# A GNN layer with a residual and a layer norm: the projected table p kept as two float32r words in place of three bfloat16 words, and its split moved from GpSimd to ScalarE and VectorE

## The chip, the cores and the metric

The kernel runs on one core of a Trainium2 chip. The metric is device time in microseconds (us), one launch, the median of the runs shown. Engines are named as in the profile: PE is TensorE (PEld its weight loads), ACT is ScalarE, DVE is VectorE, POOL is GpSimd, SP is SyncE, which here only issues DMAs.

## The reference, cut to what matters

```python
# x (12500, 256), src and dst (200000,), edge_weight (200000,), 4 heads, DO = 64
def head(w1, bb1, w2, bb2, a1, aab1, a2, aab2):
    feats = jnp.maximum(x @ w1 + bb1, 0.0) @ w2 + bb2            # (12500, 64)
    x_cat = jnp.concatenate([feats[src], feats[dst], edge_weight[:, None]], axis=1)   # 129 wide
    hid = jnp.maximum(x_cat @ a1 + aab1, 0.0)                    # (200000, 129)
    e1 = jax.nn.leaky_relu((hid @ a2 + aab2)[:, 0], negative_slope=0.2)
    w = jnp.exp(e1 - jnp.max(e1))
    pooled = segment_sum(w[:, None] * feats[dst], src)
    row_sum = segment_sum(w, src) + 1e-10
    return pooled / row_sum[:, None]
out = layernorm(x + concatenate_heads(vmap(head)(...)))
```

`x_cat @ a1` is a sum of three parts, p[src] + q[dst] + weight * a_row. With 4 heads p and q have ZW = 4 * 129 = 516 columns. p holds the bias `aab1`, and each is made once for each node and not once for each edge.

## The kernel before

**Nodes and windows.** The 12500 nodes are 100 windows of WN = 125. A table `p_table` has p, another, `qf_table`, has q and the features (QW = 776 columns, float32). Every edge belongs to the window of its source node.

**First part, to about 400 us.** Weights and edges are loaded, and the edges are counted by window.

**The sort loop (`sort_loop`, 26 groups, of which 25 make nodes).** A group is 16 steps q = 0 to 15, on each engine in an order written out by hand. It handles four blocks of 2000 edges and at the same time makes p, q and the features of four windows. For the sort, each step has on PE a prefix sum (`prefix`, L823) and placing products (`place`, L834), on ACT the one-hot rows of windows (`windows`, L1051 and L1056), on DVE `pick` (L1398) and `chunks` (L1433). Once in four steps DVE has `split` and `slots` (L1407 to L1423) and `row_ids` (L1442), and POOL scatters the rows of a block with three indirect DMAs (`scatter`, L695). For the nodes PE has `hidden` (L857, q = 1 to 8), `feats` (L866, q = 3 to 9), `q_product` (L888, q = 10 to 13) and `p_product` (L877, q = 11, 13, 15 and 1 of the group after). Both p_products of a window write psum banks 5 and 6. DVE's `p_sum` (L1454, same steps as `p_product`) adds the bias and writes p to `p_f`. POOL's `split_p` (L706 to L713) makes three bfloat16 words of it in four instructions, and SP stores them. PE's next `p_product` waits for `p_sum` of the last one:

```python
def p_product(g, w):
    ...
    since(pe, s_p_ev, n)
    for q in range(2):
        mm = pe.matmul(psum[0:WN, 5 + q, 0:HALF], f_t[:, q, at], ad_p[:, q, :], start=True, stop=True)
```

PE's order at q = 1 is prefix, turned rows, place, `p_product` of the window before, `hidden(0)`. PE may run two prefixes ahead of DVE's `pick` and no further. DVE's order in a step is split, pick, slots, row_ids, chunks, and then what stands beside.

**The tables.** After the sort, windows of tiles are packed into a table `win_pack`, `end_prev` holds where windows end, and the sorted fields are turned into `records`.

**The edge loop (`pipeline`, 208 superblocks of 8 tiles of 128 edges, 1664 tiles).** For each tile POOL gathers 128 rows of `qf_table` (L754) into one of 24 slots. PE's `hidden_src` makes p[src]: a one-hot matrix of 128 x 128 (`onehot_t`, bfloat16) times the window's p (`p_win`, three words, 258 columns at a time), so six products (L971). Then the identity times the gathered half, in float32 (L975). `turn` transposes one-hot matrices (L984, four at a time), after `hidden_src(2)` for the second half of this superblock and after `hidden_src(6)` for the first half of the next. `sum_up` (L958, float32) sums the weighted features. ACT's `take_turned` (L1182) copies the transposed matrices to `onehot_t`, twice a superblock. ACT also builds one-hot matrices (`onehots`, L1193 to L1197) and weights features (`weight`, L1164, four heads for each tile). ACT's order in a superblock is take_turned, onehots, exps, weight(0), take_turned, weight(1) to (3), weight(4), onehots, weight(5) to (7). `hidden_src(0)` and `hidden_src(4)` wait for take_turned. DVE adds p and q (L1558), has four dot products (L1568), sums up (L1617) and some small steps once a superblock (L1582 to L1624).

SP loads the p of a window while the one before it is in work (`p_win` has two places). The last 100 us are the division, the residual and the layer norm.

Of the kernel before, what the change touches and what calls it, by code (L numbers as in the profile page):

```python
# [25 lines left out]
I32 = mybir.dt.int32  # L26
BF16 = mybir.dt.bfloat16
AX_X = mybir.AxisListType.X


def gnn_layer(nc, x, src, dst, weight, W1, b1, W2, b2, A1, ab1, A2, ab2, out):
# [50 lines left out]
    p_table = nc.dram_tensor("p_table", (N, 3 * ZW), BF16, kind="Internal").ap()  # L82
# [7 lines left out]
    with ctx:  # L90
# [12 lines left out]
        ones_b = sb("ones_b", [P, P], BF16)  # L103
        before = sb("before", [P, P], BF16)
        iota_row = sb("iota_row", [P, WN])
        iota_win = sb("iota_win", [P, CH, W], BF16)
# [4 lines left out]
        onehot_t = sb("onehot_t", [P, SB, P], BF16)  # L111
# [10 lines left out]
        decay = sb("decay", [P, SPB, H])  # L122
        shift_all = sb("shift_all", [P, NSB, H])
        last_sb = sb("last_sb", [P, W], I32)
        end_prev = sb("end_prev", [1, W], I32)
        win_pack = sb("win_pack", [1, NT // 4], I32)
# [4 lines left out]
        row_tmp = onehot_t[0:1, :, :].rearrange("p t n -> p (t n)").bitcast(I32)[:, 0:NT // 4]  # L131
# [66 lines left out]
        dst_part = edge_row.bitcast(I32)  # L198
        hist_m = base_hl[:, 0:2 * HG * HCOL * LO].rearrange("p (b m c n) -> p b m c n", b=2, m=HG, c=HCOL)
# [90 lines left out]
        s_tab_step = sem("s_tab_step")  # L290
        s_acc_zero = sem("s_acc_zero")
# [191 lines left out]
        def _(sp):  # L483
# [1248 lines left out]
```

## Time and profile before

| what | value |
|---|---|
| median of 3 runs | 4876.15 us (4874.23 to 4877.1) |
| span of the profiled execution | 4828.3 us |
| median less span | 47.85 us |
| busy share PE, DVE, ACT, POOL | 88%, 92%, 79%, 56% |
| sort loop, from one group to the next | 52.3 us |
| edge loop, three superblocks | 45.27 us |

The span is the time from the first to the last instruction that the profile holds. What lies around it, start and end of the launch, is in the runs' times and not in the span; of the profiled execution only the span is on record. A busy PE isn't PE at its peak, since the end of a matmul is modelled: the distance between two starts says more than the duration.

### The profile page before, as it was taken

How to read it: one execution, taken by the hardware profiler on the slowest of the kernel's cores; microseconds unless marked ns; L12 is line 12 of the kernel's file. 1: busy time of each engine (PE TensorE's matmuls, PEld its weight loads, DVE VectorE, ACT ScalarE, POOL GpSimd, SP SyncE). 2: the span in 40 equal slices, each digit the busy share in tenths (PEclk: the TensorE clock that was granted, in tenths of full speed). 3: DMA queues.
4: the chain of work that ended last, by engine and by line, in shares of the span. 5: the costliest groups of instructions: out<-in, count | busy, mean ns of one | idle time of the engine just before them, and what ended most of it. 6: DMA issues, size and time to landing. Idle time of an engine off the chain costs nothing.

```text
span 4828.3 us, 133194 instructions
## 1 busy us (share of the span) xinstructions
PE 4260.4 (88%) x24114; PEld 3004.1 (62%) x24115; DVE 4460.2 (92%) x25378; ACT 3835.5 (79%) x12983; POOL 2693.5 (56%) x2886
## 2 busy tenths in 40 slices
PE   1598998898896999999999999999999999999990
PEld 1355555555555777777777777777777777777760
DVE  8799999999996999999999999999999999999998
ACT  1587778778774888888888888888888888888884
POOL 5366666666664555555555555555555555555544
PEclk9999999999997999999999999999999999999995
DMA  2133333333334877777777777777777777777757
GB/s 85 43 73 86 79 71 80 81 77 80 79 76 137 240 225 221 228 225 224 224 225 224 225 225 221 226 224 224 225 224 224 224 225 225 225 225 225 221 172 212
DMA packets 266918, 851.82 MB, mean 176 GB/s; under 512 B 107916, under 2 KB 109584, under 8 KB 266861
## 3 DMA queue, kind: packets, MB, share of 16 engines
q0 software_dynamic: 169920, 673.54, 50.0%
q1 hardware_dynamic: 63543, 160.18, 11.2%
q10 hardware_dynamic: 33398, 17.49, 1.4%
q8 instruction: 18, 0.29, 0.0%
q14 instruction: 39, 0.32, 0.0%
HBM read 739.10 MB, written 111.90 MB: 176 GB/s over the span
## 4 chain that ended last, share of the span: by engine, by line
PE 36%; ACT 27%; issue 3%; DVE 2%; DMA 1%; ACTq 0%; POOL 0%; DVEq 0%; SPq 0%; POOLq 0%
ACT z L1164 18%; PE psum L971 15%; PE psum L975 9%; PE psum L958 8%; ACT onehot L1193 3%; ACT onehot_t L1182 3%; PE psum L984 3%; ACT onehot L1197 2%; PE psum L939 1%; DVE z L1689 1%; DVE z L1682 0%; PE psum L995 0%; ACT onehot L1195 0%; DVE z L1705 0%; DMA p_win<-p_table 0%
## 5 line engine op out<-in xcount | busy, mean ns | idle before, releaser
L754 POOL DMA_INDIRECT z<-qf_table,rec x1664 | 1609.2, 967 | 1454.9 <-PE psum L958 1027.1
L1164 ACT ACTIVATE z<-z 128x64 f32<-128x64 f32 x6656 | 1651.1, 335 | 0.0
L971 PE MATMUL psum<-p_win,onehot_t 128*128 x9984 | 1407.8, 274 | 84.1 <-ACT onehot_t L1182 68.3
L971 PEld LDWEIGHTS psum<-p_win,onehot_t 128*128 128x128 bf16 x9984 | 966.8, 97 | 540.0 <-issue 214.4
L958 PE MATMUL psum<-z,onehot 128*128 128x260 f32 x3328 | 1029.4, 391 | 6.7 <-DVE acc L1617 4.9
L975 PE MATMUL psum<-z,ident 128*128 128x258 f32 x3328 | 1002.7, 383 | 0.0
L1568 DVE SCALAR_TENSOR_TENSOR z<-z,a_b 128x129 f32<-128x129 f32 x3328 | 884.3, 290 | 5.6 <-issue 0.2
L1568 DVE SCALAR_TENSOR_TENSOR z<-psum,a_b 128x129 f32<-128x129 f32 x3328 | 828.2, 286 | 0.0
L1558 DVE TENSOR_TENSOR z<-z,psum 128x258 f32<-128x258 f32 x1664 | 698.6, 420 | 94.6 <-PE psum L975 90.6
L1617 DVE TENSOR_TENSOR acc<-acc,psum 125x260 f32 x1664 | 702.3, 422 | 25.3 <-PE psum L958 2.4
L695 POOL DMA_INDIRECT sorted_rows<-z x300 | 478.5, 1595 | 403.9 <-DVE z L1447 321.6
L958 PEld LDWEIGHTS psum<-z,onehot 128*128 128x128 f32 x3328 | 575.8, 190 | 103.1 <-DVE acc L1617 27.7
L1182 ACT ACTIVATE onehot_t<-psum 128x512 bf16<-128x512 f32 x416 | 243.4, 585 | 437.7 <-PE psum L984 437.7
L1193 ACT ACTIVATE onehot<-iota_row,rec 128x125 f32<-128x125 f32 x1664 | 525.5, 389 | 26.3 <-PE psum L958 22.7
L1051 ACT ACTIVATE z<-iota_win,z 125x100 bf16<-125x100 bf16 x1600 | 470.3, 369 | 71.3 <-DMA base_rows<-z 56.3
L1433 DVE TENSOR_SCALAR acc<-z 125x320 bf16<-125x320 bf16 x1600 | 521.1, 388 | 0.3 <-issue 0.3
L975 PEld LDWEIGHTS psum<-z,ident 128*128 128x128 f32 x3328 | 502.2, 190 | 20.3
L857 PE MATMUL psum<-acc 128*128 128x500 f32 x800 | 377.8, 594 | 5.6 <-ACT acc L1085 5.6
L1398 DVE SCALAR_TENSOR_TENSOR z<-psum,z 125x100 f32<-125x100 f32 x1600 | 319.5, 253 | 24.1 <-PE psum L823 24.0
L984 PE MATMUL psum<-ident,onehot 128*128 128x128 f32 x1664 | 261.5, 280 | 55.7 <-ACT onehot L1197 55.7
L1197 ACT ACTIVATE onehot<-onehot,ones_f 128x500 f32<-128x500 f32 x416 | 298.2, 717 | 0.0
L1091 ACT ACTIVATE acc<-psum,acc 128x500 f32<-128x500 f32 x200 | 135.3, 676 | 196.0 <-PE psum L857 195.9
(220 smaller groups left out, 5576.3 us busy)
## 6 DMA issues: line engine op xcount, KB each, us to landing
p_table<-acc SPq DMA_DIRECT2D x100, 338.6 KB
p_win<-p_table SPq DMA_DIRECT2D x100, 338.6 KB
z<-qf_table,rec POOLq DMA_INDIRECT x1664, 4.5
qf_table<-acc SPq DMA_DIRECT2D x75, 339.5 KB
acc<-in_x_dram SPq DMA_DIRECT2D x25, 448.0 KB
z<-in_x_dram SPq DMA_DIRECT2D x20, 560.0 KB
out_dram<-z ACTq DMA_DIRECT2D x20, 560.0 KB
qf_table<-z SPq DMA_DIRECT2D x25, 339.5 KB
```

What stands on the lines that cost most here:

```text
L695: pool.indirect_dma_start(out=sorted_rows, out_offset=bass.IndirectOffsetOnAxis(ap=row_i[0:KB[k], (b - 3) % 2, k:k + 1], axis=0), in_=rows ...
L754: pool.indirect_dma_start(out=z_t[:, o + j, :], out_offset=None, in_=qf_table, in_offset=bass.IndirectOffsetOnAxis(ap=rec[:, o + j, 3:4].b ...
L958: pe.matmul(psum[:, 4 + j % 2, 0:H * HF], onehot[:, slot, :], z_t[:, slot, ZW:QW], start=True, stop=True)\
L971: mm = pe.matmul(to, onehot_t[:, j, :], p_flat[:, bass.ds((w % 2) * (3 * ZW) + (part * ZW + o), n)], start=(part == 0), stop=(part == 2 an ...
L975: mm = pe.matmul(z_two(slot), ident[:, :], z_t[:, slot, NA:ZW], start=False, stop=True, skip_group_check=True)
L1051: op = act.activation(win_oh[0:EP, b % 2, c, :], iota_win[0:EP, 0, :], ACT.Abs, scale=-1.0, bias=edge_win[0:EP, bass.ds((g * PER + b) * CB ...
L1164: op = act.activation(z_t[:, slot, o:o + DO], z_t[:, slot, o:o + DO], ACT.Copy, scale=z_t[:, slot, o + DO:o + HF])
L1193: op = act.activation(onehot[:, oo + j, 0:WN], iota_row[:, :], ACT.Abs, scale=-1.0, bias=rec[:, oo + j, 0:1])
L1433: op = dve.tensor_scalar(chunk_oh[0:EP, r, c, :], iota_k[0:EP, :], chunk_f[0:EP, c:c + 1], None, ALU.is_equal)
L1558: dve.tensor_tensor(own, own, z_one(slot), ALU.add).then_inc(s_z_added, 1)
L1568: return dve.scalar_tensor_tensor(out=own, in0=of, scalar=0.0, in1=a2_b[:, h * AT:(h + 1) * AT], op0=ALU.max, op1=ALU.mult, accum_out=e_ra ...
L1617: dve.tensor_tensor(a, a, psum[0:WN, 4 + j % 2, 0:H * HF], ALU.add).then_inc(s_acc, 1)
```

## The change

* p is stored as two float32 words: ACT copies the product from PSUM into `p_out` as float32r (`high_part`), and DVE subtracts that word from the same PSUM (`p_low`). `p_sum`, `p_f` and POOL's `split_p` go.
* The bias comes in by one more product for each half, a column of ones (one row) times the bias row, in float32.
* `high_part` is at ACT's steps q = 12, 14 and 0, 2 of the group after, behind `windows`; `p_low` last in DVE's steps of the same numbers. `p_sum` was at q = 11, 13, 15, 1.
* In the edge loop the one-hot matrix is written as float32r and p is multiplied in two words: four products for a tile in place of six.
* `p_win`, `p_table` and `onehot_t` get larger: 1032 words of 4 bytes for a node in place of 1548 of 2 bytes. To make room, `win_pack` and `end_prev` are built in z and copied by one DMA into a free row of `acc` after ACT's last zeroing of `acc`; other constants move to z.
* The row `a_row`, which stands below p in `p_win`, is split in two steps and not in five.

```diff
-        p_win = sb("p_win", [P, 2, 3 * ZW], BF16)
+        p_win = sb("p_win", [P, 2, 2 * ZW], F32R)
-        onehot_t = sb("onehot_t", [P, SB, P], BF16)
+        onehot_t = sb("onehot_t", [P, SB, P], F32R)
...
+        tables = acc[WN:WN + 1, 0:NT // 4 + W]
...
             def store_p(g, w):
-                sp.wait_ge(s_p_lo, g * 4 + w + 1)
+                sp.wait_ge(s_p_ev, g * 4 + w + 1)
...
             sp.wait_ge(s_tab_step, N_TAB_STEPS)
+            sp.wait_ge(s_acc_zero, 1 + BULK)
+            sp.dma_start(tables, tables_made).then_inc(s_tab_st, 16)
             sp.wait_ge(s_rec_st, 16 * BULK)
...
-            def split_p(g, w):
...
-                pool.tensor_copy(p_out[0:WN, b, 0:ZW], pf).then_inc(s_p_hi, 1)
...
-                pool.tensor_tensor(pf, pf, p_out[0:WN, b, 0:ZW], ALU.subtract).then_inc(s_p_rest, 1)
...
-            order = [(split_p, -1, 3), (scatter, 0, 0), (scatter, 0, 1), (scatter, 0, 2), (split_p, 0, 0), (split_p, 0, 1),
-                     (scatter, 0, 3), (split_p, 0, 2)]
...
                 for q in range(2):
-                    mm = pe.matmul(psum[0:WN, 5 + q, 0:HALF], f_t[:, q, at], ad_p[:, q, :], start=True, stop=True)
+                    pe.matmul(psum[0:WN, 5 + q, 0:HALF], f_t[:, q, at], ad_p[:, q, :], start=True, stop=False)
+                    mm = pe.matmul(psum[0:WN, 5 + q, 0:HALF], ones_f[0:1, 0:WN], ab1_b[0:1, q * HALF:(q + 1) * HALF], start=False, stop=True)
...
-                        for part in range(3):
-                            mm = pe.matmul(to, onehot_t[:, j, :], p_flat[:, bass.ds((w % 2) * (3 * ZW) + (part * ZW + o), n)],
-                                           start=(part == 0), stop=(part == 2 and not (o and PEH)), skip_group_check=True)
+                        for part in range(2):
+                            mm = pe.matmul(to, onehot_t[:, j, :], p_flat[:, bass.ds((w % 2) * (2 * ZW) + (part * ZW + o), n)],
+                                           start=(part == 0), stop=(part == 1 and not (o and PEH)), skip_group_check=True)
...
+            def high_part(g, w):
+
+                n, b = g * 4 + w, w % 2
+                act.wait_ge(s_p_mm, n + 1)
+                since(act, s_p_st[b], g * 64 + w // 2 * 32)
+                act.activation(p_out[0:WN, b, 0:ZW].bitcast(F32R).rearrange("p (q n) -> p q n", q=2), psum[0:WN, 5:7, 0:HALF], ACT.Copy).then_inc(s_p_hi, 1)
+
+            beside = {0: [(-1, high_part, 2), (0, take_x)], 1: [(0, take_h, 0)], 2: [(-1, high_part, 3), (0, take_h, 1)], 3: [(0, take_h, 2)],
+                      4: [(0, take_h, 3)], 5: [(0, take_h, 4)], 6: [(0, take_h, 5)], 7: [(0, take_f, 0), (0, take_h, 6)], 8: [(0, take_h, 7)],
+                      9: [(0, take_f, 1)], 10: [(0, take_q, 0)], 11: [(0, take_q, 1)], 12: [(0, high_part, 0), (0, take_q, 2)], 13: [(0, take_q, 3)],
+                      14: [(0, high_part, 1)]}
...
-            def p_sum(g, w):
+            def p_low(g, w):
 
                 n = g * 4 + w
-                dve.wait_ge(s_p_mm, n + 1)
-                since(dve, s_p_lo, n - 1)
-                dve.tensor_tensor(p_f[0:WN, w % 2, :].rearrange("p (q n) -> p q n", q=2), psum[0:WN, 5:7, 0:HALF],
-                                  ab1_b[0:WN, :].rearrange("p (q n) -> p q n", q=2), ALU.add).then_inc(s_p_ev, 1)
-
-            beside = {11: [(0, p_sum, 0)], 13: [(0, p_sum, 1)], 15: [(0, p_sum, 2)], 1: [(-1, p_sum, 3)]}
+                dve.wait_ge(s_p_hi, n + 1)
+                dve.tensor_tensor(p_out[0:WN, w % 2, ZW:].rearrange("p (q n) -> p q n", q=2), psum[0:WN, 5:7, 0:HALF],
+                                  p_out[0:WN, w % 2, 0:ZW].rearrange("p (q n) -> p q n", q=2), ALU.subtract).then_inc(s_p_ev, 1)
+
+            beside = {12: [(0, p_low, 0)], 14: [(0, p_low, 1)], 0: [(-1, p_low, 2)], 2: [(-1, p_low, 3)]}
```

## Rows read from the trace of the kernel before

**Rows 1.** Busy time by stage: window, length, PE, PEld, DVE, ACT, POOL, clock, DMA share, GB/s.

```profile
400.00:1480.00 1080.00, 965.76 (x3959) 552.97 (x3958) 1030.30 (x5193) 843.77 (x2280) 687.57 (x578) 0.98 0.36 79
```

**Rows 2.** The same for three superblocks of the edge loop.

```profile
3000.00:3045.27 45.27, 43.38 (x275) 32.83 (x274) 42.27 (x268) 38.77 (x145) 24.69 (x30) 1.00 0.75 220
```

**Rows 3.** Waits in the edge loop: total us, times, longest.

```profile
ACT onehot_t L1182 <- PE psum L984: 418.4, 203, 2.2
```

**Rows 4.** Timeline of the edge loop, ACT and PE: start, us, engine, line.

```profile
3002.54 0.60 ACT L1182 ACTIVATE onehot_t<-psum 128x512 bf16<-128x512 f32 x1 [2.19 <-PE psum L984]
...
3011.62 0.57 ACT L1182 ACTIVATE onehot_t<-psum 128x512 bf16<-128x512 f32 x1
...
3012.64 0.92 PE L971 MATMUL psum<-p_win,onehot_t 128*128 x6 [0.20 <-issue]
...
3014.26 0.82 PE L971 MATMUL psum<-p_win,onehot_t 128*128 x6
...
3014.93 0.60 PE L975 MATMUL psum<-z,ident 128*128 128x258 f32 x2
...
3015.36 0.60 PE L958 MATMUL psum<-z,onehot 128*128 128x260 f32 x2
...
3017.61 0.60 ACT L1182 ACTIVATE onehot_t<-psum 128x512 bf16<-128x512 f32 x1 [1.88 <-PE psum L984]
```

**Rows 5.** A group of weight loads, whole span: count, busy us, mean ns, idle before.

```profile
L975 PEld LDWEIGHTS psum<-z,ident 128*128 128x128 f32 x3328 | 502.2, 190 | 20.3
```

**Rows 6.** One DVE line from 400 to 1480 us: duration ns min/median/max.

```profile
L1433 DVE TENSOR_SCALAR acc<-z x1320: 286/298/1231, 401.1 to 1479.6; 125x320 bf16<-125x320 bf16 x189
```

**Rows 7.** Timeline of PE in the sort loop, steps q = 12 to 3.

```profile
1093.92 0.33 PE L823 MATMUL psum<-z,before 127*128 127x400 bf16 x1
...
1109.97 1.14 PE L877 MATMUL psum<-acc 128*125 128x258 f32 x4 [0.32 <-DVE acc L1454]
1110.94 1.84 PE L857 MATMUL psum<-acc 128*128 128x500 f32 x4
...
1116.73 0.33 PE L823 MATMUL psum<-z,before 127*128 127x400 bf16 x1 [1.54 <-DVE z L1398]
```

**Rows 8.** Timeline of DVE in the same steps.

```profile
1088.93 0.25 DVE L1398 SCALAR_TENSOR_TENSOR z<-psum,z 125x100 f32<-125x100 f32 x1
...
1090.51 0.25 DVE L1398 SCALAR_TENSOR_TENSOR z<-psum,z 125x100 f32<-125x100 f32 x1
...
1092.17 0.94 DVE L1433 TENSOR_SCALAR acc<-z 125x320 bf16<-125x320 bf16 x4
...
1094.73 0.16 DVE L1407 CAST z<-z 125x16 int32<-125x16 f32 x1
...
1095.49 0.26 DVE L1398 SCALAR_TENSOR_TENSOR z<-psum,z 125x100 f32<-125x100 f32 x1
...
1098.56 2.14 DVE L1433 TENSOR_SCALAR acc<-z 125x320 bf16<-125x320 bf16 x4
...
1108.37 0.94 DVE L1433 TENSOR_SCALAR acc<-z 125x320 bf16<-125x320 bf16 x4
1109.23 0.69 DVE L1454 TENSOR_TENSOR acc<-psum,acc 125x516 f32<-125x516 f32 x1
1109.83 0.16 DVE L1407 CAST z<-z 125x16 int32<-125x16 f32 x1
```

**Rows 9.** Timeline of ACT in the same steps.

```profile
1096.07 0.58 ACT L1103 ACTIVATE acc<-psum 125x516 f32<-125x516 f32 x1
...
1096.81 1.17 ACT L1051 ACTIVATE z<-iota_win,z 125x100 bf16<-125x100 bf16 x4
...
1098.58 0.60 ACT L1103 ACTIVATE z<-psum 125x516 f32<-125x516 f32 x1
```

**Rows 10.** Waits of SP's DMA queue from 1500 to 4600 us.

```profile
SPq L594 <- PE psum L975: 2238.1, 97, 28.5
SPq L596 <- DMA p_win<-p_table: 504.8, 98, 6.4
```

More of the change, by code:

```diff
@@ L27 @@
 BF16 = mybir.dt.bfloat16
+F32R = mybir.dt.float32r
 AX_X = mybir.AxisListType.X
@@ L215, in gnn_layer @@
         iota_s = carve_z(S // 2).bitcast(BF16)
+        iota_win = carve_z(W // 2).bitcast(BF16)
         ident_b = carve_z(P // 2).bitcast(BF16)
+        ones_b = carve_z(P // 2).bitcast(BF16)
+        before = carve_z(P // 2).bitcast(BF16)
         before_f = carve_z(P)
@@ L697, in scatter @@
                         in_=rows_out[0:KB[k], (b - 3) % 2, 2 * (W + 1) + k * SF:2 * (W + 1) + (k + 1) * SF], in_offset=None, compute_op=ALU.add).then_inc(s_scat, 16)
-            def split_p(g, w):
-                n, b = g * 4 + w, w % 2
-                pf = p_f[0:WN, b, :]
-                pool.wait_ge(s_p_ev, n + 1)
-                since(pool, s_p_st[b], g * 64 + w // 2 * 32)
-                pool.sem_inc(s_passed, 1)
-                pool.tensor_copy(p_out[0:WN, b, 0:ZW], pf).then_inc(s_p_hi, 1)
-                pool.wait_ge(s_p_hi, n + 1)
-                pool.tensor_tensor(pf, pf, p_out[0:WN, b, 0:ZW], ALU.subtract).then_inc(s_p_rest, 1)
-                pool.wait_ge(s_p_rest, n + 1)
-                pool.sem_inc(s_passed, 1)
-                pool.tensor_copy(p_out[0:WN, b, ZW:2 * ZW], pf).then_inc(s_p_mid, 1)
-                pool.wait_ge(s_p_mid, n + 1)
-                pool.tensor_tensor(p_out[0:WN, b, 2 * ZW:3 * ZW], pf, p_out[0:WN, b, ZW:2 * ZW], ALU.subtract).then_inc(s_p_lo, 1)
-            order = [(split_p, -1, 3), (scatter, 0, 0), (scatter, 0, 1), (scatter, 0, 2), (split_p, 0, 0), (split_p, 0, 1),
-                     (scatter, 0, 3), (split_p, 0, 2)]
             def group(g):
-                for work, off, n in order:
-                    if work is scatter and isinstance(g, int) and g * PER + n - 3 == BLOCKS - 1:
+                for n in range(PER):
+                    if isinstance(g, int) and g * PER + n - 3 == BLOCKS - 1:
                         pool.wait_ge(s_sum, 4 * BLOCKS)
                         pool.iota(win_iota, [[P, NT]], base=0, channel_multiplier=0, allow_small_or_imprecise_dtypes=True).then_inc(s_win_iota, 1)
-                    if (live_b(g, n, -3) if work is scatter else not isinstance(g, int) or 0 <= g + off < GROUPS):
-                        work(g + off, n)
+                    if live_b(g, n, -3):
+                        scatter(g, n)
             sort_loop(pool, group)
@@ L1050, in windows @@
                 for c in range(j * CH, (j + 1) * CH):
-                    op = act.activation(win_oh[0:EP, b % 2, c, :], iota_win[0:EP, 0, :], ACT.Abs, scale=-1.0,
+                    op = act.activation(win_oh[0:EP, b % 2, c, :], iota_win[0:EP, :], ACT.Abs, scale=-1.0,
                                         bias=edge_win[0:EP, bass.ds((g * PER + b) * CB + c, 1)])
@@ L1121, in group @@
                         take_rows(g, b)
-                    for work, *args in beside.get(q, []):
-                        if not isinstance(g, int) or g < GROUPS:
-                            work(g, *args)
+                    for off, work, *args in beside.get(q, []):
+                        if not isinstance(g, int) or 0 <= g + off < GROUPS:
+                            work(g + off, *args)
             act.dma_start(base_rows_d[:, :, :].rearrange("h u n -> h (u n)"), base_hl[0:BLOCKS, :].bitcast(BF16)).then_inc(s_base_st, 16)
@@ L1146, in _ @@
                                psum[:, g % 2 * 6 + 1, 0:3 * P].rearrange("p (f t) -> p t f", f=3), ACT.Copy).then_inc(s_field_b, 1)
-                act.activation(acc[:, g * part:(g + 1) * part], zero_col[:, :].to_broadcast([P, part]), ACT.Copy).then_inc(s_acc_zero, 1)
+                act.activation(acc[0:WN, g * part:(g + 1) * part], zero_col[0:WN, :].to_broadcast([WN, part]), ACT.Copy).then_inc(s_acc_zero, 1)
             act.wait_ge(s_start, 1)
```

74 lines of the change are left out of this document (31 added, 43 removed).

## The prediction

> **What bounds the kernel now.** I read the busy time by stage first, then the timelines of one cycle of each big loop, and the waits last. There are two loops, bound in two ways.
>
> The sort loop takes 52.3 us a group. In it DVE is busy 1030 of 1080 us, PE 966, ACT 844, POOL 688 [rows 1]. So DVE is the fullest engine. Part of that isn't work: `chunks` (L1433) takes 298 ns at the median and up to 1231 [rows 6]. Four of them take 0.94 us where POOL is quiet and 2.14 where the timeline has POOL in `split_p` [rows 8]. All 1320 have 431 us where 330 fours at 0.94 would have 310, so 121 us in 20.6 groups, about 5.9 us a group, nearly all of it beside GpSimd's own instructions. The group has two halves. From q = 3 to q = 11 PE runs almost without a gap (eight `hidden`, eight `feats`). From q = 12 to q = 2 DVE sets the pace and PE waits for it. With the prefix of q = 12 as zero (1093.92), the last `p_product` starts at 16.05, `hidden(0)` at 17.02 and the prefix of q = 3 at 22.81 [rows 7]. The rest to 52.3, that is 29.5 us, is PE's half.
>
> The edge loop takes 45.27 us for three superblocks, 15.09 each, with PE busy 43.4, DVE 42.3, ACT 38.8 [rows 2]. The two fullest aren't the whole story. ACT waits 203 times, 2.06 us each, for PE's `turn` (L984): once a superblock [rows 3]. That shows a cycle. From the copy L1182 at 3002.54 ACT works without a stop up to the end of the next one at 3012.19 (9.65 us). PE then starts `hidden_src(4)` at 3012.64, and three tiles and a `turn` later ACT's next copy starts at 3017.61 (4.97 us) [rows 4]. Together it is 15.07 us, the whole superblock. What makes PE's part shorter shortens the superblock, up to DVE's 42.27 / 3 = 14.09 us busy.
>
> **Edge loop: four products in place of six.** Six bfloat16 products of 258 columns take 0.67 us from start to start (3014.26 to 3014.93), 0.11 each. A float32 product of 258 columns is two matmuls and takes 0.43 (3014.93 to 3015.36) [rows 4]. No float32r product is in the trace. Below it is bounded by the bfloat16 price, 0.11, since the columns have to stream; above by the float32 one, 0.43; between them lies one float32 matmul of the two, 0.215. I take 0.11: a word that holds part of float32's digits, two of which are to give the whole, asks for one pass like a bfloat16 word, of which three give the whole. A four-byte weight load is 190 ns long [rows 5], but two of them and their two matmuls fit into 0.43, so a load hides behind 0.215 at least.
>
> So 4 x 0.11 = 0.44 for 0.67, 0.22 less a tile. In the cycle stand three tiles of PE's part, 3 x 0.22 = 0.66, which gives 14.4. DVE's 14.09 busy leaves 0.3 for its own gaps, so I take 14.5: 0.59 x 205 superblocks = 121 us less. Bounds of this term: 137 less, if all of 0.66 is had; 60 less, if DVE's waits stay; with 0.215 for a product, three tiles are 3 x 0.2 longer, which gives 15.7 and 125 us more; with 0.43 PE has 1.05 us more a tile, and 1700 us are added.
>
> The Trainium skill speaks against my price ("TensorE: Matmul & The Clock Gate", sections on back-to-back gaps, weight loads and fast weight load): the distance of matmuls in a real stream comes from load and matmul together, a load of 128 columns takes about 107 ns, the fast load isn't for FP32, and loads overlap running matmuls only in other row groups. If load and stream added up, four products would take some 0.86 us in place of 0.43, an estimate from that page. The trace disagrees for float32, where pairs with loads take 0.43 and would take more.
>
> ACT's copy to `onehot_t` reads 512 float32 columns as before; 125 x 516 written as float32 take 0.58 [rows 9], this one as bfloat16 0.57 to 0.60 [rows 4]: nothing. The window's p is a third larger. SP's load takes 504.8 / 98 = 5.15 us and is waited for by SP alone, which before that waits 2238 / 97 = 23 us for PE to be through with a window [rows 10]. 6.9 us still fit; if a window were short, 1.7 us more would show. Nothing.
>
> **Sort loop: what goes.** POOL's four instructions, and with them most of the 5.9 us of stretched `chunks`. POOL's scatters stay and stretch some. The stores wait for DVE now, later by less than a step.
>
> **Sort loop: what comes.** PE: two one-row products of 258 columns for each `p_product`. Columns count, so 0.43 each, 0.86 a `p_product` and 3.4 a group (bounds 0 and 1.14, the whole L877 group [rows 7]). DVE: `p_low` is as wide as `p_sum`, 0.60 from start to start [rows 8]. ACT: `high_part`, 0.50 to 0.58 as L1103 [rows 9]. But where they stand matters more. `p_product` waits for `p_low` of the last one, which stands a step later than `p_sum` did and behind ACT. I walk DVE's half again, prefix of q = 12 at zero, with quiet prices: split 0.76, pick and slots 3.07 (1095.49 to 1098.56), chunks 0.86, pick and row_ids 1.66 (1090.51 to 1092.17), a plain step 1.58 [rows 8]; windows 1.77, take_q 0.74 [rows 9].
>
> * q = 12: pick at 0.4, chunks end 4.3, `p_low(0)` 4.9. ACT: `high_part` delays take_q by 0.5, and `q_product(3)` runs 3.65 to 5.05. So `p_product(1)` 5.05 to 6.8.
> * PE's prefix of q = 14 is behind it. DVE's q = 13 ends at 6.5, so it waits until 7.2, ends the step at 8.8 and waits for `high_part(1)`, which ACT reaches at 8.5. `p_low(1)` ends at 9.7, `p_product(2)` at 11.5.
> * DVE: q = 15 ends at 12.2, q = 0 with split, pick, slots and chunks at 16.9, `p_low(2)` at 17.5. Only then comes `p_product(3)`, 17.55 to 19.3. Before it started at 16.05. Behind it on PE are `hidden(0)` (to 21.0), the prefix of q = 2, and `hidden(1)`.
> * The prefix of q = 3 comes at 23.4; before 22.81, where it waited 1.54 for DVE, and that wait goes.
>
> PE's half has `p_product(0)`, 0.86 longer: 29.5 + 0.86 = 30.3. The group is 53.7 us. I add 0.2 for scatters that still stretch DVE: 53.9, so 1.6 more a group, in 24 groups 38 us more. The freed DVE time isn't used because PE waits in the middle of the steps, not at their ends. Bounds: PE's busy time before is 966 / 1080 x 52.3 = 46.8 us a group [rows 1]; if the group shrank to that, it would be 132 us less in all. With two of the hops a microsecond later each, 85 more.
>
> For the stretching, the Trainium skill ("SBUF — State Buffer", who interferes with whom) says VectorE and GpSimd share a port pair which the one that comes first holds whole. The trace agrees: 2.14 for 0.94. `p_low` reads PSUM and one SBUF operand, which by that page doesn't contend.
>
> **The rest.** The copy of the tables is issued when ACT's last zeroing ends, ahead of the load of the first records, which waits for their store; I put 1 us. The split of `a_row` has three steps less under other waits: nothing, 1 us if it weren't.
>
> **The sum** against the profiled execution: 4828.3 - 121 + 38 + 1 = 4746. Median less span is 47.85, as before: 4794, some 82 us or 1.7% less than the median of 4876.15.
>
> **The rivals.**
>
> 1. *The sort loop gains too.* For it: DVE is fullest there, and 5.9 us a group go. Against: the walk above, in which PE waits for `p_low(2)`. If DVE's relief let PE run without waits, PE's 46.8 + 3.4 = 50.2 us would be the group, 2.1 less, and the time 4876 - 121 - 50 = 4705; at the bound of 46.8 it would be 4623.
> 2. *float32r costs one float32 matmul or more* (slower). Place: L971, four times a tile. For it: operands are four bytes wide and the weight load is 190 ns. Against: only that a word with part of the digits should need one pass. From 0.165 us a product on, four cost as much as six. At 0.215: 4876 + 125 + 39 = 5040; at 0.43 some 6600.
> 3. *The edge loop doesn't shorten.* Something else holds 15 us, as DVE's busy 14.09 with its waits for `turn` and maxima, or the loads of four-byte weights just eat the gain. For it: DVE is within 7%. Against: ACT's regular wait for PE [rows 3]. Then 4876 + 39 = 4915.
>
> **How the numbers follow.** My forecast 0.62, by itself 4740 to 4860; rival 1 0.13; rival 2 0.12; rival 3 0.13. A tenth of the forecast's own range would be within 0.2% or slower. Less than 0.2%, 10 us, I count as the same, about what a measurement of this kernel can tell from no change. Faster: 0.13 + 0.58 + 0.02 of rival 3 = 0.73; same 0.06; slower 0.21. Left out of the range are rival 2, the upper part of rival 3 and the far end of rival 1: 4680 to 4890. Its upper end takes in the forecast with both terms at their worse bounds within reason (60 less and 85 more, with 1, would be 4902).
>
> **What would show it.** L971 four times a tile at 0.11 from start to start, 14.5 us a superblock, ACT's wait for L984 down by about 0.6 and DVE's for L975 near zero. In the sort loop `chunks` back at 0.94 for four, groups of 53.9 us, and PE's L877 waiting for DVE's `p_low` by microseconds at q = 1, where before it was 0.32 [rows 7]. Wrong would be: a start-to-start of L971 of 0.2, groups below 51 us, or DVE idle in the edge loop by more than 0.5 us a superblock.

## The result and the profile after

The changed kernel takes 5002.77 us (median of 4 runs, 4999.77 to 5004.83) where the kernel before takes 4875.31. The ratio is 1.0259, 95% interval 1.0244 to 1.0273: slower by 127 us. The forecast was 4794, its range 4680 to 4890, and it gave "slower" a chance of 0.21.

First the page of the changed kernel: its span, the busy time of each engine, and three of its costliest groups.

```profile
span 5000.4 us, 123442 instructions
PE 4248.6 (85%) x21186; PEld 3034.1 (61%) x21187; DVE 4276.9 (86%) x25375; ACT 3879.0 (78%) x13083; POOL 2365.6 (47%) x2486
L958 PE MATMUL psum<-p_win,onehot_t 128*128 x6656 | 1351.7, 325 | 150.5 <-issue 94.3
L1393 DVE SCALAR_TENSOR_TENSOR z<-psum,z 125x100 f32<-125x100 f32 x1600 | 320.9, 256 | 371.5 <-PE psum L809 368.4
L1428 DVE TENSOR_SCALAR acc<-z 125x320 bf16<-125x320 bf16 x1600 | 382.2, 302 | 0.8 <-issue 0.8
```

What was meant to go went: POOL is busy 47% of the span, and `chunks` (now L1428) takes 302 ns on average and four of them 0.94 us again. But `pick` (now L1393) waits 368 us for PE's prefix. The same two stretches as in [rows 1, 2] say where the time came from. The columns are busy times of PE, PEld, DVE, ACT, POOL, the granted clock, DMA share, GB/s.

```profile
400.00:1480.00 1080.00, 994.61 (x3699) 532.58 (x3698) 768.94 (x4483) 776.52 (x2060) 353.37 (x216) 0.92 0.33 76
3000.00:3045.27 45.27, 40.78 (x234) 32.98 (x232) 43.09 (x273) 39.82 (x150) 25.51 (x32) 1.00 0.79 237
```

In the sort loop DVE does 4483 instructions in the time in which it did 5185 to 5193, and PE has the lower granted clock, 0.92. A group takes 60.9 us (median of 24, mean 60.6) for 52.3 before: about 195 us more in 24 groups. The edge loop is shorter: 14.74 us a superblock (median) for 15.08. Here is the place in the sort loop, the timeline of PE from the prefix of q = 12 of one group to that of q = 3 of the next (L809 is `prefix`, L863 and L864 are `p_product` and its bias rows, L843 is `hidden`):

```profile
1054.99 0.34 PE L809 MATMUL psum<-z 127*128 127x400 bf16 x1
...
1060.05 0.70 PE L863 MATMUL psum<-acc 128*125 128x258 f32 x2 [0.76 <-DVE acc L1448]
1060.68 0.70 PE L864 MATMUL psum<-acc,ones_f 1*125 1x258 f32 x2
...
1062.56 0.34 PE L809 MATMUL psum<-z 127*128 127x400 bf16 x1
...
1065.27 0.70 PE L863 MATMUL psum<-acc 128*125 128x258 f32 x2 [0.54 <-DVE acc L1448]
...
1073.79 0.88 PE L863 MATMUL psum<-acc 128*125 128x258 f32 x2 [3.42 <-DVE acc L1448]
...
1078.05 3.40 PE L843 MATMUL psum<-acc 128*128 128x500 f32 x4
1081.28 0.33 PE L809 MATMUL psum<-z 127*128 127x400 bf16 x1
...
1083.69 0.33 PE L809 MATMUL psum<-z 127*128 127x400 bf16 x1
```

The reader is to see three things. `p_product(1)` with its bias takes 2.51 us from start to start (1060.05 to 1062.56). The last one waits 3.42 us for `p_low(2)` (L1448). After this wait it takes 4.26 us, and `hidden(0)` 3.23, where before the same four matmuls took 1.68. The same stretches in the view by windows (the granted clock is the third column from the end):

```profile
1054.00:1074.00 20.00, 15.27 (x75) 8.90 (x75) 15.99 (x82) 15.47 (x42) 8.42 (x6) 1.00 0.49 122
1074.00:1084.50 10.50, 10.50 (x27) 4.88 (x27) 2.99 (x22) 2.98 (x9) 0.00 (x0) 0.67 0.20 52
1084.50:1114.50 30.00, 29.80 (x113) 15.79 (x111) 24.22 (x149) 25.92 (x70) 11.69 (x8) 1.00 0.29 57
```

PE is busy for all of the second stretch, but at 1.2 GHz for about two thirds of it. Summed over 24 groups, PE's clock stands at this lower level for 236 us, 10.2 us in most groups and 6.8 in the one shown, which with 59.55 us is one of the shortest. All of it lies between the prefix of q = 12 and that of q = 3. In the first profile of before it is 55 us in all, 3.4 us in two groups of three, and these groups are no longer than the third (52.1 to 52.4 us, one 52.9, for 52.2 to 52.4): there DVE sets the pace.

### The profile page after: what moved, and what is told of

Read it like the earlier page. It is cut to its first block, busy times and chain, and to the rows that moved or that the text cites. A ratio compares the mean times of both kernels' runs of the same rounds, so it can differ in the third digit from the quotient of the medians.

```text
span 5000.4 us, 123442 instructions
## 1 busy us (share of the span) xinstructions
PE 4248.6 (85%) x21186; PEld 3034.1 (61%) x21187; DVE 4276.9 (86%) x25375; ACT 3879.0 (78%) x13083; POOL 2365.6 (47%) x2486
## 4 chain that ended last, share of the span: by engine, by line
ACT 31%; PE 22%; issue 6%; DVE 4%; ACTq 1%; another core or an unknown queue 1%; DMA 0%; DVEq 0%; POOL 0%; POOLq 0%; SPq 0%
ACT z L1159 19%; PE psum L958 7%; ACT onehot L1188 6%; PE psum L945 5%; PE psum L962 5%; PE psum L971 3%; ACT onehot_t L1177 3%; ACT onehot L1192 2%; DVE z L1555 1%; DVE z L1545 1%; PE psum L926 1%; PE psum L982 1%; DVE z L1676 1%; ACT onehot L1190 0%
## 5 line engine op out<-in xcount | busy, mean ns | idle before, releaser
L958 PE MATMUL psum<-p_win,onehot_t 128*128 x6656 | 1351.7, 325 | 150.5 <-issue 94.3
L958 PEld LDWEIGHTS psum<-p_win,onehot_t 128*128 128x128 f32 x6656 | 1007.0, 189 | 410.5 <-issue 334.1
L945 PE MATMUL psum<-z,onehot 128*128 128x260 f32 x3328 | 1036.5, 393 | 36.8 <-issue 19.7
L700 POOL DMA_INDIRECT sorted_rows<-z x300 | 494.0, 1647 | 1069.8 <-DVE z L1442 910.9
L962 PE MATMUL psum<-z,ident 128*128 128x258 f32 x3328 | 999.2, 381 | 0.0
L945 PEld LDWEIGHTS psum<-z,onehot 128*128 128x128 f32 x3328 | 568.9, 190 | 156.8 <-issue 74.2
L1393 DVE SCALAR_TENSOR_TENSOR z<-psum,z 125x100 f32<-125x100 f32 x1600 | 320.9, 256 | 371.5 <-PE psum L809 368.4
L1177 ACT ACTIVATE onehot_t<-psum 128x512 fp32r<-128x512 f32 x416 | 243.9, 586 | 416.8 <-PE psum L971 289.2
L1038 ACT ACTIVATE z<-z 125x100 bf16<-125x100 bf16 x1600 | 470.0, 369 | 59.9 <-DMA base_rows<-z 56.3
L962 PEld LDWEIGHTS psum<-z,ident 128*128 128x128 f32 x3328 | 516.2, 190 | 0.3 <-DMA z<-qf_table,rec 0.3
L843 PE MATMUL psum<-acc 128*128 128x500 f32 x800 | 418.1, 648 | 5.6 <-ACT acc L1072 5.6
L1428 DVE TENSOR_SCALAR acc<-z 125x320 bf16<-125x320 bf16 x1600 | 382.2, 302 | 0.8 <-issue 0.8
L971 PEld LDWEIGHTS psum<-ident,onehot 128*128 128x128 f32 x1664 | 192.6, 141 | 267.2 <-ACT onehot L1192 236.5
```

What stands on the lines that cost most here:

```text
L700: pool.indirect_dma_start(out=sorted_rows, out_offset=bass.IndirectOffsetOnAxis(ap=row_i[0:KB[k], (b - 3) % 2, k:k + 1], axis=0), in_=rows ...
L945: pe.matmul(psum[:, 4 + j % 2, 0:H * HF], onehot[:, slot, :], z_t[:, slot, ZW:QW], start=True, stop=True)\
L958: mm = pe.matmul(to, onehot_t[:, j, :], p_flat[:, bass.ds((w % 2) * (2 * ZW) + (part * ZW + o), n)], start=(part == 0), stop=(part == 1 an ...
L962: mm = pe.matmul(z_two(slot), ident[:, :], z_t[:, slot, NA:ZW], start=False, stop=True, skip_group_check=True)
L971: mm = pe.transpose(psum[:, 6, j * P:(j + 1) * P], onehot[:, ((k + off) * SB + u * HALF_SB + j) % RING, :], ident[:, :])
L1038: op = act.activation(win_oh[0:EP, b % 2, c, :], iota_win[0:EP, :], ACT.Abs, scale=-1.0, bias=edge_win[0:EP, bass.ds((g * PER + b) * CB + ...
```

## The experiments

**Theory A**: the group grew for two reasons that the sum did not hold. A product with one row of weights is dearer than its columns, and PE's wait for `p_low(2)`, which the new order of the words brings, lets the clock fall. **The rivals**: the split is simply too much work for ACT and DVE; or the time is PE's added work alone; or waiting, not the clock, is what costs. In the short diffs below, "-" is the changed kernel unless another is named. "Half clock" is the time that PE's granted clock is at 1.2 GHz, summed over 24 groups of the sort loop, from the first prefix of q = 12 on. (The expectations of e10 and e11 name 255 and 205 us where this table has 236 and 181: they count from some 20 us ahead of the loop's first prefix, where PE's clock is low in some profiles and not in others; e8, which has the sort loop of e2, has it there, and e2 hasn't.)

| kernel | median us | ratio to before, 95% interval | group, median us | half clock us |
|---|---|---|---|---|
| before, profiled twice | 4875 | 1 | 52.3; 52.4 | 55; 68 |
| after | 5002.77 | 1.0259 (1.0244 to 1.0273) | 60.9 | 236 |
| e1, no bias rows | 4848.29 | 0.9940 (0.9924 to 0.9957) | 54.6 | 164 |
| e2, words early | 4783.52 | 0.9807 (0.9791 to 0.9823) | 51.8 | 0 |
| e3, hidden first | 4940.93 | 1.0129 (1.0113 to 1.0146) | 57.8 | 181 |
| e4, bias by 128 rows | 4881.69 | 1.0008 (0.9998 to 1.0018) | 55.3 | 109 |
| e5, words by POOL | 4768.23 | 0.9768 (0.9752 to 0.9785) | 50.9 | 48 |
| e6, before with bias rows | 4932.81 | 1.0106 (1.0089 to 1.0123) | 54.4 | 75 |
| e7, early and 128 rows | 4734.60 | 0.9701 (0.9685 to 0.9717) | 49.8 | 0 |
| e8, early, one word | 4745.20 | 0.9727 (0.9711 to 0.9743) | 51.8 | 0 |
| e10, wait filled | 4891.74 | 1.0046 (1.0029 to 1.0063) | 56.4 | 3 |
| e11, hidden first, filled | 4851.72 | 0.9965 (0.9951 to 0.9979) | 54.6 | 3 |
| e12, early, in pairs | 4740.81 | 0.9738 (0.9721 to 0.9754) | 50.6 | 0 |

The last batch (e9 to e12) ran on a chip on which before took 4869.46 us, the others where it took 4875 to 4879; so ratios are what is compared across batches.

**e1_no_bias.** It leaves out the bias of p.

```diff
-pe.matmul(psum[0:WN, 5 + q, 0:HALF], f_t[:, q, at], ad_p[:, q, :], start=True, stop=False)
-mm = pe.matmul(psum[0:WN, 5 + q, 0:HALF], ones_f[0:1, 0:WN], ab1_b[0:1, q * HALF:(q + 1) * HALF], start=False, stop=True)
+mm = pe.matmul(psum[0:WN, 5 + q, 0:HALF], f_t[:, q, at], ad_p[:, q, :], start=True, stop=True)
```

> The changed kernel without the one-row products; the bias ab1 is left out of p. In the changed kernel a group of the sort loop takes 60.7 us, a p_product with its bias 2.51 us from start to start, and PE waits 3.4 us before the last p_product, after which its clock is at half for 10 us. Theory A, three causes that add up (price of the one-row products, the late place of high_part and p_low, the clock that falls in that wait): p_product falls to 0.86 us, the wait before the last one grows to about 4.5 us, the clock still falls; the group is about 54.5 us and the time about 4855. Theory B, the late place alone is the cause and the one-row products cost what their columns cost: 3.4 us a group less, about 4920. Theory C, the loss isn't in p's handling at all: within 20 us of 5003.

Measured: 4848 us, the group 54.6. The rows cost 3.2% of the time, 154 us, far more than the 82 us (24 x 3.4) that the sum had for them. Part of that is the clock, whose half clock fell from 236 to 164 us. These 164 us stay, and the group is still above the 52.3 of before: the bias is not the only cause.

**e2_early.** `high_part` and `p_low` stand one step earlier, each directly behind its `p_product`.

```diff
-ACT: 0: [(-1, high_part, 2), ...], 2: [(-1, high_part, 3), ...], 12: [(0, high_part, 0), ...], 14: [(0, high_part, 1)]
+ACT: 1: [(-1, high_part, 3), ...], 11: [..., (0, high_part, 0)], 13: [..., (0, high_part, 1)], 15: [(0, high_part, 2)]
-DVE: {12: [(0, p_low, 0)], 14: [(0, p_low, 1)], 0: [(-1, p_low, 2)], 2: [(-1, p_low, 3)]}
+DVE: {11: [(0, p_low, 0)], 13: [(0, p_low, 1)], 15: [(0, p_low, 2)], 1: [(-1, p_low, 3)]}
```

> high_part and p_low at the steps q = 11, 13, 15 and 1, where p_sum was; all else as changed. Theory A: p_low(2) ends about 4 us earlier in relation to the prefix of q = 12, PE doesn't wait before the last p_product, the clock stays at full, and the group is about 52.5 us with the one-row products still in; time about 4800. Theory B, that the one-row products are the cause: the group stays above 58 us, time above 4940. Theory C: within 20 us of 5003.

Measured: 4784 us, 4.4% less than the changed kernel, and no half clock at all. The work of all engines is the same as after, so "too much work for ACT and DVE" falls: only the place of two instructions turned a kernel that is slower than before by 2.6% into one that is faster by 1.9%.

**e3_hidden_first.** PE does `hidden(0)` ahead of the last `p_product`.

```diff
-beside = {1: [(-1, p_product, 3), (0, hidden, 0)], ...
+beside = {1: [(0, hidden, 0), (-1, p_product, 3)], ...
```

> At q = 1 PE does hidden(0) before the last p_product and not after it; all else as changed. Theory A: hidden(0), 1.7 us, fills half of the wait of 3.4 us; the wait left is under 2 us, the clock stays at full, which gives 3.4 us back, and 1.7 us of the wait are used: the group is about 55.6 us, time about 4880. If the clock fell for another reason than this wait: the granted clock in the sort loop stays near 0.92 and the gain is 40 us at most, time about 4960. Theory C: within 20 us of 5003.

Measured: 4941 us, near the alternative and 61 us above theory A's own number. The timeline of PE shows why:

```profile
1091.05 1.84 PE L843 MATMUL psum<-acc 128*128 128x500 f32 x4
1094.63 0.70 PE L863 MATMUL psum<-acc 128*125 128x258 f32 x2 [1.74 <-DVE acc L1448]
1095.26 0.70 PE L864 MATMUL psum<-acc,ones_f 1*125 1x258 f32 x2
1095.88 1.22 PE L863 MATMUL psum<-acc 128*125 128x258 f32 x2
1097.04 1.22 PE L864 MATMUL psum<-acc,ones_f 1*125 1x258 f32 x2
1098.19 0.52 PE L809 MATMUL psum<-z 127*128 127x400 bf16 x1
1098.50 1.27 PE L820 MATMUL psum<-acc,z 125*96 125x320 bf16 x4
1099.56 3.40 PE L843 MATMUL psum<-acc 128*128 128x500 f32 x4
```

`hidden(0)` fills only 1.68 us. 1.74 us of waiting stay, and behind them the clock falls all the same. I had taken it that half the wait would not be enough for that; whether this wait is its cause was open, and e11 tests it.

**e4_full_rows.** The bias product has 128 rows of weights (`ab1_b` is zero but for row 0) and the same columns.

```diff
-mm = pe.matmul(psum[0:WN, 5 + q, 0:HALF], ones_f[0:1, 0:WN], ab1_b[0:1, q * HALF:(q + 1) * HALF], start=False, stop=True)
+mm = pe.matmul(psum[0:WN, 5 + q, 0:HALF], ones_f[:, 0:WN], ab1_b[:, q * HALF:(q + 1) * HALF], start=False, stop=True)
...
```

> The bias product over all 128 rows (a matrix of ones times a tile whose first row is the bias and whose others are zero) in place of one row; same sum. In the changed kernel each float32 product of 258 columns around a one-row product takes 0.63 us, alone it took 0.43. If the change of row count is what keeps the weight load from being hidden: 0.43 again, p_product with bias 1.73 us, the group 3 us shorter, about 57.5 us, time about 4925. If it is the accumulation of two products in one bank, or anything else: 0.63 stays and the time is within 20 us of 5003.

Measured: 4882 us, 2.4% less than after, for more weights. The direction is theory A's. The size is above it because half clock also fell from 236 to 109 us.

**e5_pool_words.** No bias rows. DVE adds the bias as before, in the early steps, and POOL makes the two words in two instructions, in its order of before.

```diff
+dve.tensor_tensor(p_f[...], psum[0:WN, 5:7, 0:HALF], ab1_b[...], ALU.add).then_inc(s_p_sum, 1)
...
+pool.tensor_copy(p_out[0:WN, b, 0:ZW].bitcast(F32R), pf).then_inc(s_p_hi, 1)
+pool.tensor_tensor(p_out[0:WN, b, ZW:2 * ZW], pf, p_out[0:WN, b, 0:ZW], ALU.subtract).then_inc(s_p_ev, 1)
```

> The two-word edge loop as changed, but p's handling as before: no one-row product, p_sum adds the bias on DVE at q = 11, 13, 15 and 1, and POOL makes the two float32r words in two instructions in place of four. Theory A (the sort loop lost by PE's price and by the places): PE is as before, DVE is stretched by about half as much as before, the group is 51 to 52 us, the edge loop is that of the changed kernel (14.74 us a superblock at the median, 15.0 in the mean), time about 4755 to 4785. If the changed edge loop or its tables had cost anything on their own: above 4850.

Measured: 4768 us, as expected, with the group at 50.9 just under my 51 to 52. This is the change without its new steps on PE and ACT, and gives 111 us: 1.5 us a group in 24 groups (two POOL instructions less for each of four windows), and the shorter edge loop.

**e6_before_rows.** The kernel before, with the one-row product added (the bias is then in p twice).

```diff
-mm = pe.matmul(psum[0:WN, 5 + q, 0:HALF], f_t[:, q, at], ad_p[:, q, :], start=True, stop=True)
+pe.matmul(psum[0:WN, 5 + q, 0:HALF], f_t[:, q, at], ad_p[:, q, :], start=True, stop=False)
+mm = pe.matmul(psum[0:WN, 5 + q, 0:HALF], ones_f[0:1, 0:WN], ab1_b[0:1, q * HALF:(q + 1) * HALF], start=False, stop=True)
```

> The kernel before with the one-row products alone added to p_product (p_sum still adds the bias, so it counts twice in p). Theory A: a p_product goes from 0.86 to 2.5 us; the one at q = 11 stands in PE's half and adds 1.65 us to the group, those in DVE's half add less; the group is 54 to 55.5 us in place of 52.3, time 4915 to 4950. If their columns alone counted (0.86 each): 53.2 us, about 4895. If the waits hid them: within 10 us of before.

Measured: 4933 us, 53 more, with the clock hardly touched (half clock 75 us for 55 to 68). So the rows alone cost about 2.1 us a group.

**e7_early_full.** e2 and e4 together.

> e2_early and e4_full_rows together: high_part and p_low at q = 11, 13, 15, 1 and the bias product over 128 rows. Theory A: p_product is 1.73 us and not 2.51; with the clock already at full in e2_early only PE's half gains, 0.8 us a group and perhaps as much again in the other half: 50.5 to 51.3 us, time 4745 to 4765 where e2_early had 4784. If the 121 us that the full rows gave before came from the clock alone: within 8 us of e2_early.

Measured: 4734.6 us, 3.0% faster than before, a little more than expected, and the best of all. The two timelines of PE, first e2 and then e7, have the price of the rows without the clock in it (both at full clock):

```profile
1048.26 0.60 PE L863 MATMUL psum<-acc 128*125 128x258 f32 x2
1048.79 0.69 PE L864 MATMUL psum<-acc,ones_f 1*125 1x258 f32 x2
1049.41 0.70 PE L863 MATMUL psum<-acc 128*125 128x258 f32 x2
1050.04 0.69 PE L864 MATMUL psum<-acc,ones_f 1*125 1x258 f32 x2
1050.67 1.95 PE L843 MATMUL psum<-acc 128*128 128x500 f32 x4
```

```profile
1054.44 0.60 PE L863 MATMUL psum<-acc 128*125 128x258 f32 x2
1054.88 0.60 PE L864 MATMUL psum<-acc,ones_f 128*125 128x258 f32 x2
1055.31 0.60 PE L863 MATMUL psum<-acc 128*125 128x258 f32 x2
1055.75 0.60 PE L864 MATMUL psum<-acc,ones_f 128*125 128x258 f32 x2
1056.18 0.33 PE L809 MATMUL psum<-z 127*128 127x400 bf16 x1
```

With one row the four products take 2.41 us (2.51 when the product before was a one-row one too), 0.63 each in the middle; with 128 rows they take 1.74, 0.43 each. The product with 127 more rows of weights is the cheaper one.

**e8_one_word.** e2, and the edge loop leaves the low word of p out (two products a tile in place of four).

```diff
-for part in range(2):
+for part in range(1):
...
```

> e2_early with only the high word multiplied in the edge loop (the low word of p is left out): two products a tile. If PE's part of the cycle with ACT still sets the edge loop: three tiles 0.33 us shorter each would give 13.75 us a superblock, and DVE's 14.05 busy is the floor, so 14.2 to 14.4 at the median, and the time 70 to 110 us under e2_early's 4784. If DVE or ACT alone already sets it at 14.74: within 20 us of e2_early. Stretches that are longer than the median (15 to 17 us, every eleventh superblock or so) stay if they come from something other than the products.

Measured: 4745 us, 38 less than e2, which lies between my two cases (70 to 110, or within 20). A superblock is 14.62 us for 14.75, nearer to the second case: PE's products no longer set it. The page of windows shows what is fullest now: DVE is busy 44.04 of 45.27 us.

```profile
3000.00:3045.27 45.27, 38.16 (x184) 25.86 (x183) 44.04 (x275) 40.42 (x150) 25.54 (x32) 1.00 0.80 246
```

**e9_before_again.** The kernel before, unchanged, profiled a second time.

> The kernel before, profiled a second time. My sum took 47.85 us outside the span as a constant, but every other kernel had 2 to 4 us there. Theory C: the first profiled execution of before lacked stalls of the edge loop that its timed ones have. Then this span is 4870 to 4880 us, the superblock's median stays at 15.1 us and its mean rises from 15.12 to about 15.35, as in the kernel of before with the bias rows added. Rival: 48 us lie outside the span of this kernel in every execution; then the span is 4828 again and the mean 15.12.

Measured: 4866.58 us with a span of 4864.8, so 1.8 us outside it. The span is 5 us under my 4870 to 4880, and the timed runs of before on this chip have 4869.46. Theory C holds: the superblock's median is again 15.08 us, its mean 15.29 (15.12 in the first profile).

**e10_filled.** PE computes `hidden(0)` twice for nothing while it waits at q = 1.

```diff
+def again(g, m):    # the waits and the four matmuls of hidden, no signal
-beside = {1: [(-1, p_product, 3), (0, hidden, 0)], ...
+beside = {1: [(0, again, 0), (0, again, 0), (-1, p_product, 3), (0, hidden, 0)], ...
```

> The changed kernel, but in PE's wait of 3.4 us at q = 1 it computes hidden(0) twice over for nothing (2 x 1.68 us), before the last p_product; the real hidden(0) follows as it did. The wait for p_low stays as long as it is, only PE no longer stands still in it. Theory A (the group's half clock follows from PE standing still and costs about 3.4 us a group): half-clock time in the sort loop falls from 255 us to under 60, the group from 60.9 to 57.0 to 57.8, the time to 4915 to 4935. Rival (waiting alone costs, the clock is a by-product): the group stays at 60.5 to 61, the time at 4995 to 5010.

Measured: ratio 1.0046 for 1.0259, so 104 us less by 3.4 us more of work in each group; the group 56.4 (4.5 less, more than the 3.1 to 3.9 that I expected), half clock 3 us for 236. The rival falls. The last `p_product` still starts 13.75 us after `p_product(1)` (13.74 in after), so `p_low(2)` comes as late as it did. The wait for it is now filled, and what stands behind it runs at full clock (L852 is the tail of `again`):

```profile
1069.71 2.68 PE L852 MATMUL psum<-acc 128*128 128x500 f32 x6
1072.46 0.70 PE L871 MATMUL psum<-acc 128*125 128x258 f32 x2
...
1074.97 1.95 PE L843 MATMUL psum<-acc 128*128 128x500 f32 x4
1076.76 0.33 PE L809 MATMUL psum<-z 127*128 127x400 bf16 x1
```

The granted clock from 400 to 1480 us, the columns as above:

```profile
400.00:1480.00 1080.00, 1050.11 (x4134) 566.64 (x4133) 826.71 (x4826) 832.74 (x2225) 372.85 (x229) 1.00 0.36 82
```

**e11_first_filled.** e3, with one more `again` (into the free bank of `hidden`) ahead of `p_product`.

```diff
-beside = {1: [(0, hidden, 0), (-1, p_product, 3)], ...
+beside = {1: [(0, hidden, 0), (0, again, 1), (-1, p_product, 3)], ...
```

> The kernel with hidden(0) ahead of the last p_product, where 1.7 us of waiting and 205 us of half clock were left, and in that wait one more product of four matmuls for nothing (1.68 us, in the free bank of hidden). Theory A: half-clock time under 80 us, the group from 57.8 to 55 to 56, the time from 4941 to 4885 to 4905. Rival (the clock there fell for another reason, as the 0.8 us wait at q = 14): half-clock time stays near 200 and the time at 4935 to 4950.

Measured: ratio 0.9965 for 1.0129 (80 us less), half clock 3 us for 181, the group 54.6 for 57.8. So it was the remaining wait of 1.7 us that e3's clock fell for. The gain is above my number here too.

**e12_early_pairs.** e2, with the two products of 128 rows first and the two of one row after them.

```diff
 for q in range(2):
     pe.matmul(psum[0:WN, 5 + q, 0:HALF], f_t[:, q, at], ad_p[:, q, :], start=True, stop=False)
+for q in range(2):
     mm = pe.matmul(psum[0:WN, 5 + q, 0:HALF], ones_f[0:1, 0:WN], ab1_b[0:1, q * HALF:(q + 1) * HALF], start=False, stop=True)
```

> The early order of the words (4784 us, group 51.8), with the two products of 128 rows first and the two of one row behind them, so that the rows of the weights change twice a p_product and not four times. Theory A1 (the change of rows costs): p_product from 2.5 to 2.1 us, the group to 50.8 to 51.0, the time to 4758 to 4768. Theory A2 (each product with one row costs by itself, 0.4 us a pair): the group 51.8, the time 4780 to 4788.

Measured: ratio 0.9738 for 0.9807, about 34 us less, of which some 15 are seen in the edge loop, which isn't edited (3086 us for 3101, on another chip); the group 50.6 for 51.8. The timeline:

```profile
1062.46 1.03 PE L863 MATMUL psum<-acc 128*125 128x258 f32 x4
1063.42 1.13 PE L865 MATMUL psum<-acc,ones_f 1*125 1x258 f32 x4
1064.49 0.34 PE L809 MATMUL psum<-z 127*128 127x400 bf16 x1
```

2.03 us for 2.41 to 2.51: the same products in another order. So most of the extra price is in the change of rows and not in the one-row product by itself. That both products of a half go to the same bank isn't it, since they do so in e7 as well. Between 1.74 and 2.03 about 0.3 us stay for two changes.

## Why the prediction was wrong

**The clock, a term that the sum lacked: about 4.5 us a group.** The walk had the wait. It put `p_product(3)` at 17.55 us after the prefix of q = 12, and named "PE waiting for `p_low(2)`" as what would show. It came at 18.80 (1054.99 to 1073.79) with a wait of 3.42 us. What the walk didn't have is that the matmuls behind such a wait cost twice as much. It has `p_product(3)` and `hidden(0)` at 1.75 and 1.7 us; they took 4.26 and 3.23. The prefix of q = 3 was forecast at 23.4 and came at 28.70. These 5.3 us are 1.25 before `p_product(3)`, 2.5 in it (0.8 of them the price below) and 1.5 in `hidden(0)`. e10 gives the clock's whole part: 4.5 us a group, with the wait left where it was.

The Trainium skill ("TensorE: Matmul & The Clock Gate", Part 1 and its table of terms) says that the array's default is half the clock, that activity lifts it and standing idle brings it back, and that the penalty is the throttled time x (1 - 1/2). The runs agree about: from after to e10 half clock fell by 232 us, half of which is 116, and 24 x 4.5 = 109 us of group time went. This page stood in the prediction for the weight loads, and its first part would have been the term that was missing.

**The price of the one-row products, mis-sized: 2.51 us in place of 1.73.** "Columns count, so 0.43 each" was the step. Two such products added 1.54 us to a `p_product` (2.51 less 0.97), outside the bounds that I gave (0 and 1.14). The upper bound came from a group of four matmuls that all have 128 rows. Alternation was in no row of before, and the bound for an unseen operation reached only to its own size. Against 128 rows this cost 2.0 us a group in the early order (e2 and e7), where other waits take up a part, and 5.6 in the changed kernel (e4). There 126 us less of half clock, halved and shared among 24 groups, are 2.6 of the 5.6, and 3.0 are left, about 4 x 0.78.

**What is left of the walk was right.** The forecast had 1.6 us a group more. Of the measured 8.6, the clock has 4.5, the rows' extra price about 3.1 (4 x 0.78), and 1.0 is left. DVE's relief came, and was not used, as forecast: PE waits in the middle of the steps. PE's half, from the prefix of q = 3 to that of the next q = 12, is 30.85 us in every group of after (here 1083.69 to 1114.54) for 30.3, and 0.7 more is just `p_product(0)` (2.40, 1052.59 to 1054.99, for 1.73). It is 30.85 in e2 and e10 too, so all else that after lost stands in DVE's half. That half is 28.7 us in the group shown and 30.2 at the median, since the clock is low for longer in most groups.

**The edge loop: the mechanism right, the size 0.34 a superblock for 0.59.** The price of a float32r product was nearly right. Starts overlap with what is before, so I take the stretch from `sum_up` (L945, 0.43 by itself) to the float32 product L962, which holds the products of p:

```profile
3018.77 0.60 PE L945 MATMUL psum<-z,onehot 128*128 128x260 f32 x2
3019.02 0.84 PE L958 MATMUL psum<-p_win,onehot_t 128*128 x4
3019.70 0.60 PE L962 MATMUL psum<-z,ident 128*128 128x258 f32 x2
3020.13 0.60 PE L945 MATMUL psum<-z,onehot 128*128 128x260 f32 x2
3020.38 0.84 PE L958 MATMUL psum<-p_win,onehot_t 128*128 x4
```

That is 0.93 less 0.43, so 0.50 for four, 0.125 each, where I had 0.44. A tile takes PE 1.36 us (3019.02 to 3020.38) for 1.54 before, which makes 0.54 in the three tiles of PE's part. Two steps on the way to this price were weak, though it came right. The row on float32 pairs didn't speak against load and stream adding up, as the prediction has it: with the 0.215 that it then puts for a load and a stream, a pair takes just the 0.43 of that row. And its time at 0.215 a product counts three tiles of a superblock, where PE would have had eight (14.46 us busy and 8 x 0.2, about 16.1 us, not 15.7). Only 0.34 of the 0.54 was had, since DVE became the bound. Its timeline in the middle of a superblock:

```profile
3017.59 0.42 DVE L1545 TENSOR_TENSOR z<-z,psum 128x258 f32<-128x258 f32 x1
...
3019.11 0.41 DVE L1545 TENSOR_TENSOR z<-z,psum 128x258 f32<-128x258 f32 x1
...
3020.63 0.41 DVE L1545 TENSOR_TENSOR z<-z,psum 128x258 f32<-128x258 f32 x1
...
3022.15 0.41 DVE L1545 TENSOR_TENSOR z<-z,psum 128x258 f32<-128x258 f32 x1
```

A tile takes DVE 1.52 us without any gap, and PE, which needs 1.36, now runs into DVE. I had given DVE 0.3 us of gaps on top of its busy 14.09. It has 0.7 (14.74 less 14.03 busy), 0.68 of it one wait for the maxima. e8 shows that it isn't the products any more: half of them left out moves a superblock by 0.13 us. ACT's wait before its copy, which was to fall by 0.6, fell by about 0.24 (2.07 us before, 1.83 after, each the mean from 1800 to 4650 us). The term was 121 us; it is 0.34 x 207 = 70, and 61 by the length of the loop (3103.5 us after, 3164.6 in e9).

**Median less span, a constant that wasn't one.** I added 47.85 us to the span of the changed kernel. In every other run it is under 5 us, and in the second profile of before 1.8. The two profiles of before differ in the edge loop. The first has 1.5 us in superblocks that are over 0.3 above the median (summed, what is above it), that of e9 31 and that of after 52. So 4828 is not what a timed run of before looks like. It did no harm to the forecast, which came out as the median plus the differences.

**The sum again**, with e9 as before: 24 x (60.63 - 52.58) = +193, the edge loop 3103.5 - 3164.6 = -61, the way from sort to edge loop and the end +3 together: 135 us, for 5000.4 - 4864.8 = 136. With the forecast's terms it was +38, -121 and +1. The sign turned on the first term, of which the rivals held nothing: my case for "slower" was the price of float32r, and that price was right. That a wait which I had found could change the speed of what follows it was not among the rivals.

**What stays open.** The edge loop of every kernel but the first profile of before has a slow superblock about every 165 us (in after 17.01 us at 2143.9, 16.41 at 2308.2, 15.80 at 2471.5), in which engines start late with their releaser long done. The rows of after at the first of them:

```profile
2146.28 0.60 PE L945 MATMUL psum<-z,onehot 128*128 128x260 f32 x2
2147.63 0.42 DVE L1545 TENSOR_TENSOR z<-z,psum 128x258 f32<-128x258 f32 x1 [1.68 <-PE psum L962]
2148.86 0.85 PE L958 MATMUL psum<-p_win,onehot_t 128*128 x4 [1.98 <-DVE z L1555]
```

No instruction was fetched by DMA there, and the trace doesn't name a cause. e6, with its bfloat16 words, has them too, so they aren't the change's. That is argued from traces and was not tested by a run of its own.

## What to carry to other kernels

When a walk through the queues ends in a wait of TensorE, price what stands behind it at half the clock, as well as the wait, wherever TensorE is what the others then wait for. Here waits of 1.7 or 3.4 us in a group of 60 cost 3 to 4.5 us through the clock, beside their own length, and either placing the releaser a step earlier (4.4%, the wait itself included) or filling the wait with useless matmuls (2.1%) won it back. A helper that has few rows can be dearer than a full one: compare it with the same product padded to 128 rows, or at least group the thin ones. And before a shortened stage is priced, look at how far the next engine stands from the bound in that stage, gaps included; take a second profile as soon as a span and the median differ by 1%.

## What the runs showed of the hardware that was not expected

* A float32 product of 258 columns with 1 row of weights, between products with 128 rows, takes 0.63 us, and so does the product with 128 rows between two such; with 128 rows 0.43 (e2, e7). In pairs, 1, 1 after 128, 128, they take 0.48 to 0.54 each (e12).
* A float32r product of 258 columns takes about 0.125 us in a stream, the loads of its four-byte weights included; a bfloat16 one 0.11, a float32 one 0.43.
* PE's clock fell to 1.2 GHz after a wait of 3.42 us in after and after one of 1.74 us in e3, and the matmuls behind it took 3.23 us for 1.68. In e2, e7 and e12, where nothing holds PE up at that place, it stayed at 2.4 GHz through the 24 groups.
